# Merging partition tails into the stored state rows before the two graph merges

## What is computed

```python
x = x + gat_both_directions(layernorm(x), src, dst)      # 4 heads x 32 per direction, self loop, fused by W_fuse, batch norm, relu
x = x + top2_of_8_experts(layernorm(x))
x = x + edge_attention(layernorm(x), src, dst, edge_attr)  # 8 heads x 32, softmax over the edges that enter a node
x = x + slice_attention(layernorm(x))                    # 8 heads x 64 slices
```

## Time and profile before

| | us |
|---|---|
| median of 3 runs | 6456.18 |
| the profiled execution | 6453.75 |
| its span, first to last instruction | 6452.0 |
| layer 0: `join_tails` | 2584.9 to 2598.4 |
| layer 0: `combine` | 2598.4 to 2890.3 |
| layer 1: `edge_pass` | to 5835.8 |
| layer 1: `join_tails` | 5840.4 to 5852.5 |
| layer 1: `combine` | 5852.5 to 5962.6 |
| `slice_attention`, weights | 5962.6 to 5992.4 |
| `slice_attention`, slice loop | 5992.4 to about 6300 |

### The profile page before, as it was taken

How to read it: one execution, slowest core, us unless ns; L and a number is a source line. 1 busy time by engine, 2 the same in 40 slices (tenths; PEclk the granted TensorE clock), 3 DMA queues, 4 the chain that set the end, 5 groups by cost and what they waited for, 6 DMA issues and landing times. The chain is left out here.

```text
span 6452.0 us, 53855 instructions
## 1 busy us (share of the span) xinstructions
PE 3055.3 (47%) x13342; PEld 2333.7 (36%) x13342; DVE 4201.4 (65%) x8039; ACT 1470.0 (23%) x2631; POOL 3252.6 (50%) x3330
## 2 busy tenths in 40 slices
PE   4613200000000000447888585777777777773777
PEld 3512100000000000335555333666666666662456
DVE  3747778882455555575333354999999999997563
ACT  2013323331333333111222100222222222221230
POOL 0067767775777776423312244666666666664000
PEclk9555555555555555666999797888888888886798
DMA  2123353331453333213222225999999999992013
GB/s 84 46 61 102 108 165 109 109 108 49 127 190 110 110 109 99 72 47 112 98 66 81 60 108 163 282 282 282 286 282 283 282 282 284 284 284 64 28 46 138
DMA packets 291974, 948.60 MB, mean 147 GB/s; under 512 B 84065, under 2 KB 124904, under 8 KB 250277
## 3 DMA queue, kind: packets, MB, share of 16 engines
q0 software_dynamic: 167056, 470.20, 26.2%
q1 hardware_dynamic: 124772, 476.82, 21.6%
HBM read 625.98 MB, written 332.57 MB: 149 GB/s over the span
## 5 line engine op out<-in xcount | busy, mean ns | idle before, releaser
L1241 PE MATMUL e_psE<-e_we,e_eaT 128*128 128x256 f32 x3136 | 941.9, 429 | 440.8 <-DMA e_kv<-kv,rec 434.5
L793 POOL DMA_INDIRECT g_g<-t,rec x784 | 775.4, 989 | 281.4 <-issue 280.8
L1107 POOL DMA_INDIRECT e_kv<-kv,rec x784 | 774.8, 988 | 245.4 <-issue 245.4
L1241 PEld LDWEIGHTS e_psE<-e_we,e_eaT 128*128 128x128 f32 x3136 | 672.5, 218 | 575.8 <-issue 452.4
L793 POOL DMA_INDIRECT g_g<-t,dst_of x784 | 740.1, 944 | 260.0 <-issue 257.3
L1100 POOL DMA_INDIRECT e_q<-q,q_of x392 | 381.0, 972 | 462.7 <-DVE e_at L1141 341.8
L1347 PE MATMUL j_psM<-ident,tail 128*128 128x128 f32 x32 | 7.5, 429 | 1195.3 <-PEq L53 1195.3
L1242 PE MATMUL e_psE<-e_kv,ident 128*128 128x256 f32 x1568 | 523.2, 419 | 0.0
L829 DVE TENSOR_TENSOR_SCAN g_wv<-g_fx,g_wv 128x2176 f32<-128x2176 f32 x98 | 459.0, 4684 | 0.4 <-issue 0.4
L1347 PEld LDWEIGHTS j_psM<-ident,tail 128*128 128x128 f32 x32 | 7.0, 330 | 1196.0 <-issue 1196.0
L804 DVE TENSOR_TENSOR g_at<-g_g,ar 128x64 f32<-128x64 f32 x98 | 26.2, 267 | 627.3 <-DMA g_g<-t,dst_of 461.3
(11 more groups left out here) (496 smaller groups left out, 6847.7 us busy)
## 6 DMA issues: line engine op xcount, KB each, us to landing
state<-e_st SPq DMA_DIRECT2D x98, 1088.0 KB, 5.7
e_ea<-in_edge_attr SPq DMA_DIRECT2D x98, 896.0 KB, 9.9
state_f<-g_st SPq DMA_DIRECT2D x49, 1088.0 KB, 4.3
state_b<-g_st SPq DMA_DIRECT2D x49, 1088.0 KB, 4.3
m_work<-xs SPq DMA_DIRECT2D x119, 128.0 KB, 2.2
ys<-m_work SPq DMA_DIRECT2D x119, 128.0 KB, 1.7
xs<-g_zeros SPq DMA_DIRECT2D x28, 512.0 KB
g_g<-t,rec POOLq DMA_INDIRECT x784
```

The source lines that it names most:

```text
L793: pool.indirect_dma_start(g[:, u, j, :], None, tab, bass.IndirectOffsetOnAxis(ap=at_, axis=0)).then_inc(gat[u], 16)
L1107: pool.indirect_dma_start(kv[:, u, b, :], None, c.kv, bass.IndirectOffsetOnAxis(ap=c.rec[:, t, 1:2], axis=0)).then_inc(gkv[u][b // 4], 16)
L1241: nc.tensor.matmul(half, eaT[:, m, j, k, :], we[:, k, :], start=(k == 0), stop=False)
```

## The change

- `join_tails` writes its result to the state tables. POOL gathers, for each partition's key, the number of the row (`rowof`, from `c.ends`) and then the row itself; VectorE merges it with the tails' sum; POOL scatters the merged row back (partitions without a key write to spare rows, for which the tables grow by 128 rows). `carry` and `fkey` go.
- `combine(c, 0)` becomes `combine_directions(c)`: no one-hots, no carries; two parts to merge instead of three; the batch norm's scale is folded into the fusion weight and its shift, with the bias of the two directions, into a row that TensorE adds with a third product per tile; six accumulator tiles in place of two; group g + 1 is weighed ahead of group g's fusion; POOL reads the row numbers without a copy and is not told to wait for the weights.
- `combine(c, 1)` goes. Its division and addition to `x` are done by `receive` inside the slice loop, ahead of the wait on `acc`; the gathers are POOL's in that loop.
- `join_tails(c, 1)` is called inside `slice_attention` with a function that issues its loads (12 and the row numbers) from SP during the join.

```diff
 def join_tails(c, layer, other_loads=None):
@@ sync
+            if other_loads is not None:
+                other_loads(sp)
             sp.wait_ge(nl, 16 * nd)
+        @block.gpsimd
+            nc.gpsimd.iota(nth[:], ...).then_inc(counted, 1)
+            pool.wait_ge(keyed, 1)
+            for d in range(nd):
+                pool.indirect_dma_start(rowof[:, d:d + 1], None, ends, ...kidx[:, d:d + 1]).then_inc(found, 16)
+            pool.wait_ge(found, 16 * nd)
+            for d in range(nd):
+                pool.indirect_dma_start(row[:, d, :], None, states[d][0:EP + 1, :], ...rowof[:, d:d + 1]).then_inc(fetched, 16)
+            pool.wait_ge(joined, 1)
+            for d in range(nd):
+                pool.indirect_dma_start(states[d], ...rowto[:, d:d + 1], new[:, d, :], None).then_inc(stored, 16)
+            pool.wait_ge(stored, 16 * nd)
@@ vector
-            ts(c.fkey[:, 0:nd], first[:], 1.0, None, ALU.subtract)
+            ts(none[:], first[:], 0.5, None, ALU.is_lt)
+            ts(first[:], first[:], 1.0, None, ALU.subtract)
+            v.drain()
+            nc.vector.scalar_tensor_tensor(out=kidx[:], in0=none[:], scalar=float(KEYS), in1=first[:], ...).then_inc(keyed, 1)
...
+            v.wait_ge(fetched, 16 * nd)
+            tt(rowto[:], rowof[:], none[:], ALU.add)
+            tt(new[:, :, wd + hd:rest], row[:, :, wd + hd:rest], tops, ALU.max)
+            v.drain()
+            tt(both[:, 0], row[:, :, wd + hd:rest], new[:, :, wd + hd:rest], ALU.subtract)
+            tt(both[:, 1], tops, new[:, :, wd + hd:rest], ALU.subtract).then_inc(weighed, 1)
             v.wait_ge(gd, 1)
+            v.wait_ge(powers, 1)
             for d in range(nd):
-                copy(g[:, d, 0:wd + hd], psG[d][:, 0:wd + hd])
-                copy(g[:, d, wd + hd:wd + 2 * hd], top[:, d * hd:(d + 1) * hd])
-            nc.vector.memset(g[:, :, wd + 2 * hd:wd + 2 * hd + 1], 1.0)
+                tt(heads(new[:, d, 0:wd]), heads(row[:, d, 0:wd]), by(0, C), ALU.mult)
+                tt(new[:, d, wd:wd + hd], row[:, d, wd:wd + hd], both[:, 0, d], ALU.mult)
+                tt(heads(part[:, d, 0:wd]), heads(psG[d][:, 0:wd]), by(1, C), ALU.mult)
+                tt(part[:, d, wd:wd + hd], psG[d][:, wd:wd + hd], both[:, 1, d], ALU.mult)
+            v.drain()
+            tt(new[:, :, 0:wd + hd], new[:, :, 0:wd + hd], part[:], ALU.add).then_inc(joined, 1)

-def combine(c, layer):
+def combine_directions(c):
+        psF = [pb(f"psF{n}") for n in range(GT - 1)]
+        home = lambda j: psF[j % (GT - 1)][:, 0:D]
@@ gpsimd
+            pool.wait_ge(ends_in, 32)
+            for g in range(NG):
+                if g >= 2:
+                    pool.wait_ge(used, g - 1)
+                for d in range(2):
+                    for j in range(GT):
+                        pool.indirect_dma_start(rows[:, g % 2, d, j, :], None, c.state0[d][0:EP + 1, :],
+                                                ...endn[:, d, g * GT + j:g * GT + j + 1]).then_inc(got[g % 2], 16)
@@ vector
+            def weigh(g, par):
+                v.wait_ge(got[par], turns(g, par, 2 * GT * 16))
+                v.wait_ge(own_in[par], turns(g, par, 32))
+                tt(eself[:], o[:, :, :, P:P + HH], o[:, :, :, P + HH:TW], ALU.add)
+                nc.vector.scalar_tensor_tensor(out=eself[:], ..., scalar=0.2, ..., op1=ALU.max)
+                tt(top[:], best, eself[:], ALU.max)
+                tt(xa[:, 0], best, top[:], ALU.subtract)
+                tt(xa[:, 1], eself[:], top[:], ALU.subtract).then_inc(xd, 1)
+                v.wait_ge(fd, g + 1)
+                tt(dsum[:], r[:, :, :, P:P + HH], xa[:, 0], ALU.mult)
+                tt(dsum[:], dsum[:], xa[:, 1], ALU.add)
+                ts(dsum[:], dsum[:], 1e-16, None, ALU.add)
+                nc.vector.reciprocal(dsum[:], dsum[:])
+                for n in range(2):
+                    tt(xa[:, n], xa[:, n], dsum[:], ALU.mult)
+                for d in range(2):
+                    tt(hk(num_[:, :, d * P:(d + 1) * P]), hk(r[:, d, :, 0:P]), by(0, d), ALU.mult)
+                    tt(hk(tmp[:, :, d * P:(d + 1) * P]), hk(o[:, d, :, 0:P]), by(1, d), ALU.mult)
+                v.sem_inc(used, 1)
+                tt(num_, num_, tmp[:], ALU.add).then_inc(catd, 1)
+            def fuse(g):
+                for j in range(GT):
+                    v.wait_ge(mm, g * GT + j + 1)
+                    nc.vector.scalar_tensor_tensor(out=xj, in0=home(j), scalar=0.0, in1=xj, op0=ALU.max, op1=ALU.add).then_inc(fs, 1)
+            def step(g, par, ahead):
+                if ahead:
+                    weigh(g + 1, 1 - par)
+                fuse(g)
+            over_groups(v, weigh, step)
@@ scalar
+            def step(g, par, ahead):
+                if ahead:
+                    exps(g + 1, 1 - par)
+                for j in range(GT):
+                    act.wait_ge(tr, g * GT + j + 1)
+                    nc.scalar.activation(cT[:, :, j * P:(j + 1) * P], psT[j % 2]..., ACT.Copy).then_inc(tc, 1)
@@ tensor
+                for j in range(GT):
+                    pe.wait_ge(tc, g * GT + j + 1)
+                    pe.wait_ge(fs, ...)
+                    nc.tensor.matmul(home(j), ones_row(c), beta[0:1, :], start=True, stop=False)
+                    for k in range(2):
+                        last = nc.tensor.matmul(home(j), cT[:, k, j * P:(j + 1) * P], wf[:, k, :], start=False, stop=(k == 1))

 def slice_attention(c):
+        join_tails(c, 1, loads)
@@ second block, gpsimd
+                for g in range(NG):
+                    if g >= 2:
+                        pool.wait_ge(sent_used, g - 1)
+                    for j in range(GT):
+                        pool.indirect_dma_start(sent[:, g % 2, j, :], None, c.state1[0:EP + 1, :], ...).then_inc(sent_in[g % 2], 16)
@@ second block, vector
+                def receive(g, par):
+                    v.wait_ge(sent_in[par], turns(g, par, GT * 16))
+                    ts(share[:], sent[:, par, :, DEN:MX], 1e-30, None, ALU.max)
+                    nc.vector.reciprocal(share[:], share[:])
+                    tt(heads(per[:]), heads(sent[:, par, :, 0:D]), share..., ALU.mult).then_inc(sent_used, 1)
+                    tt(xg, xg, per[:].rearrange("p i d -> p (i d)"), ALU.add)
                 def prepare(g, par):
+                    receive(g, par)
                     normalize_group(c, v, w, xln[:, par], g, vin, root, xr)
                     logits(g, par)
                 def step(g, par, ahead):
                     if ahead:
+                        receive(g + 1, 1 - par)
                         v.wait_ge(acc, g + 1)
@@ build
-        join_tails(c, 1)
-        combine(c, 1)
```

More of the change, by code:

```diff
@@ L1267, in join_tails @@
         junk = sb("junk", [P, nd, P])
+        states = c.state0 if layer == 0 else [c.state1]
+        rest = wd + 2 * hd
+        none, nth, kidx, rowof, rowto = sb("none", [P, nd]), sb("nth", [P, 1]), sb("kidx", [P, nd], I32), sb("rowof", [P, nd], I32), sb("rowto", [P, nd], I32)
+        row, new = sb("row", [P, nd, rest]), sb("new", [P, nd, rest])
+        both, part = sb("both", [P, 2, nd, hd]), sb("part", [P, nd, wd + hd])
         mrow = sb("mrow", [P, H, P])
@@ L1321, in _ @@
             v.drain()
-            ts(c.fkey[:, 0:nd], first[:], 1.0, None, ALU.subtract)
+            ts(none[:], first[:], 0.5, None, ALU.is_lt)
+            ts(first[:], first[:], 1.0, None, ALU.subtract)
+            v.drain()
+            nc.vector.scalar_tensor_tensor(out=kidx[:], in0=none[:], scalar=float(KEYS), in1=first[:], op0=ALU.mult,
+                                           op1=ALU.add).then_inc(keyed, 1)
+            v.wait_ge(counted, 1)
+            ts(none[:], none[:], nth[:, 0:1], None, ALU.mult)
             v.wait_ge(fd, 1)
@@ L1400, in combine @@
         block = s.enter_context(nc.Block())
+        home = lambda j: psF[j % (GT - 1)][:, 0:D]
         @block.sync
         def _(sp):
[L1404 to L1416, removed]
-                                     tab.rearrange("(p i) w -> p (i w)", i=NI)[:, bass.ds(g * (GT * TW), GT * TW)]).then_inc(tl[par], 16)
-                over_groups(sp, lambda g, par: None, step)
@@ new lines, in _ @@
+            for tile, name in ((bfuse, "b_fuse"), (mean, "run_mean"), (var, "run_var"), (gamma, "gamma"), (beta, "beta")):
+                sp.dma_start(tile[:], row_bcast(A["L0_gnn_" + name], 0, D)).then_inc(ld, 16)
+            with nc.allow_non_contiguous_dma("one word per partition"):
+                for k, name in enumerate(("L0_gnn_b_f", "L0_gnn_b_b")):
+                    sp.dma_start(bcol[:, k:k + 1], A[name].rearrange("(p a) -> p a", a=1)).then_inc(ld, 16)
+            load_own(1, 1)
@@ new lines, in _ @@
+            ts(var[:], var[:], BN_EPS, None, ALU.add).then_inc(var_in, 1)
+            v.wait_ge(var_out, 1)
+            nc.vector.reciprocal(var[:], var[:])
+            tt(bfuse[:], bfuse[:], mean[:], ALU.subtract)
+            v.drain()
+            tt(gamma[:], gamma[:], var[:], ALU.mult)
```

(17 more changed lines are left out.)

320 lines of the change are left out of this document (120 added, 200 removed).

## The result

The changed kernel takes **6308.7 us**, the median of four runs (6304.3 to 6309.6), beside 6455.3 for the kernel before in the same runs: 0.9773 of it, 95% interval 0.9757 to 0.9790. That is 2.3% faster where 3.0% was forecast, and 6.7 us above the range. The profiled spans differ by 144.2 us (6452.0 and 6307.8); the sum had 194.7.

A forecast was written before the change was run, and what follows sets the result against it. No engine was taken as full: VectorE and TensorE alternate in a chain in the layer-0 merge and slice loop. Terms over barrier-separated stretches summed to -194.7 us, giving 6261 us against the median, range 6234 to 6302.

The forecast's parts named there:

- TensorE's fusion in the layer-0 merge: Layer-0 merge: third product priced like the other two, 1.29 us a tile, 9.0 us for seven.
- POOL's pace: Layer-0 merge: POOL's 14 gathers set the pace, 20.2 us a group, stage 173.5 us, gain 118.4.
- TensorE sets the pace: Rival, layer-0 merge: TensorE at the lower clock throughout, step 25.1 us, stage 218, whole 6305; chance 0.12.
- The argument against it: Layer-0 merge: TensorE's busy share per step rises, and present groups end at 0.86 us a tile despite 9 us idle.
- The estimate by the rule of the Trainium skill: Layer-0 merge: gathers not stretched by VectorE's wide work, 17.7 us a group; as a rival 6246 us, chance 0.06.
- Joins: Layer-0 and layer-1 joins: chained gathers and scatters make them longer, +13.5 and +9.9 us.
- Weight block: Block before the slice loop: weights already landed during the join, so TensorE's 10.5 us wait goes, -10.5 us.
- The first receive: Slice loop, group 0: gathers and receive delay the first normalization, +15.4 us.
- Group 1's receive: Slice loop: no wait to fill, but 1.3 us of waiting for the exponential goes, +3.8 us.
- the slow tiles: Slice loop: TensorE idles longer before group 0, first tiles may run at 1.2 GHz, +1.7 us (0 to +6).
- Receives of groups 2 to 6: Slice loop: 5.0 us each fill VectorE's 6.69 us wait, cost 0; rival that they are not hidden, 6286, chance 0.08.
- The slower case through the edge pass: Edge pass: larger state tables shift others and lower DMA rate; at 15% longer the whole is 6544 us; chance 0.02.

The follow-up runs named there:

- the late receive: Slice loop's receive of group g + 1 moved behind the wait for TensorE's sums, against the changed kernel; 6336.4 us.

## Why the prediction missed, step by step

**The step that failed is TensorE's fusion in the layer-0 merge.** "A third makes 1.29, so 9.0 for seven" priced the one-row product like the others, with the tile of before, 0.86 us, as the base. With 128 rows that is right at the upper clock level (1.29 measured). With one row the tile is 1.69 there: the product costs 0.83 us, outside its stated bound of nothing to 0.43. And in six of seven groups the tile was 3.15 us, in two parts. At the lower level three products of 128 rows would be 2.58 (twice 1.29); the switches between shapes add 0.57. And the level stayed the lower one: in each tile 1.43 of 3.15 us went by without a full product (two of them are 1.72, twice 0.86), which the runs below vary. By an estimate from these rows the level counts most: at the upper one seven tiles of 1.69 and the transposes of 4.17 are 16.0 us, still under POOL's 19.8, and POOL would have stayed the pace. The runs that bear on this:

| kernel | tile, lower level, us | of it without full product | tile, upper level, us | granted clock, stretches before the last group | granted clock, whole stage |
|---|---|---|---|---|---|
| third product with 128 rows | 2.58 | 0 | 1.29 | 0.67 to 0.84 | 0.75 |
| one row, 8 columns | 2.52 | 0.80 | 1.37 | 0.63 to 0.70 | 0.68 |
| no third product, one accumulator | 2.70 | 0.98, of it 0.62 idle | not seen | 0.54 to 0.59 | 0.54 |
| one row, 128 columns | 2.73 | 1.01 | 1.47 | 0.50 to 0.54 | 0.55 |
| one row, 256 columns (the change) | 3.15 | 1.43 | 1.69 | 0.50 | 0.53 |
| the kernel before with one row | 3.15 | 1.43 | 1.69 | 0.50 to 0.67 | 0.53 |
| 64 rows, 256 columns | 3.15 | 1.43 | 1.69 | 0.50 to 0.54 | 0.55 |

What is shown: with the same order of work and the same result, the change of 1 row into 128 takes 54.7 us from the stage and brings back the tile, the clock and POOL's pace of the forecast. What keeps the clock low is not shown. The versions with more time per tile without a full product have the lower clock, but this is an order of a few versions, most run once, and no rule: the switch is part of each such stretch, the one accumulator brings other waits along, and in the last group the change held the upper level for 15 us with 1.69 us tiles.

Of such products the Trainium skill says (TensorE: Matmul & The Clock Gate, Why this matters for your kernels) that a single product with 32 rows takes as long as one with 128. The trace agrees nearly: its record is 1.22 us long with one row and with 64, and 1.06 with 128 at the same level. By that rule the tile would be 1.29 at the upper level, as forecast; the trace goes against it with 1.69, by the switches around the product.

**The rival that came true** was "TensorE sets the pace", 6305 us with a chance of 0.12. It had the mechanism, TensorE at the lower level. Its price, a step of 25.1 and a stage of 218 against 27.5 and 223.4, is near partly by luck: the seven tiles took 22.1 us where it had 17.9, as it knew no switches, and the rest of the group 5.4 where it had 7.2. The argument against it, that the busy share rises and so the clock, failed: the busy share rose to 37 to 38 of 40 us, and the clock fell to 0.50. The row to distrust was there: no row of the kernel before shows a product of one row, and the bound "between nothing and the same as the others" took in its duration alone, and too little of it, not the clock.

**POOL's pace was right where it is the pace.** With 128 rows a group takes 19.76 us (five from 2655.88 to 2754.66) against 20.2 forecast, with gathers of 1.70 and 1.75 us beside VectorE's products of two inputs. The run with one more wide operation a group shows another 0.69 us. The estimate by the rule of the Trainium skill (SBUF — State Buffer, Who interferes with whom) was 17.7, and the trace goes against it with these numbers. The stage of the 128-row version, 168.7, is 4.8 under the forecast, and its whole, 6257.0, 4 under the 6261.

**The other terms.** Joins: +14.7 and +11.0 for 13.5 and 9.9; the excess is behind the last scatter, from whose beginning 3.8 us pass to the next stage in both joins (from 2612.54 and 5802.86), for 2.4 forecast. Weight block -10.6 for -10.5. The first receive +15.7 for +15.4. Group 1's receive and the slow tiles together: from the first normalization to the third 77.8 us instead of 72.3, +5.5 for +5.5; how that divides between the two was not tested. Receives of groups 2 to 6: nothing, as forecast, and the late receive shows it. The slower case through the edge pass did not come (busy DMA share 0.90 of 1884 us, against 0.91 of 1886).

## What to carry to other kernels

Where TensorE is or may become the bound, a bias product of one row is worth a test against two others, which both were faster here: filled up with rows of 1/128, or the bias added on an engine that has time. A price taken from a stage at a mixed clock holds only if the new stage keeps the same clock, so a range must hold the stage priced at each of the two levels, and a new shape of product is a reason to give the slower one real weight. Before a wait is called cover, ask what stands there if it is used; here it bore a receive of 5 us for nothing, and one line moved shows what it was worth.

## What the runs showed of the hardware that was not expected

- With a one-row product in each tile TensorE was busy in 37 to 38 of 40 us and was granted 0.50 for six groups, and 1.00 in the last one with the same products; with only 21 to 22 of 40 us busy in products of 128 rows it had 0.76.
- 64 rows and 1 row behave alike: 3.15 us a tile at the lower level, 1.69 at the upper, clock 0.50 to 0.54 before the last group.
- Going from a product of 128 rows to one of 1 or 64 and back costs 0.57 us a tile at the lower level (3.15 less 2.58) and 0.40 at the upper (1.69 less 1.29), and the weight loads show it as 0.65 us without a releaser.
